# An attention kernel on one core: twelve score visits per unit become ten, with the fills and row visits placed anew

## The chip, the cores and the metric

One core of a Trainium2 chip. The metric is the device time of one launch in microseconds; the kernel before takes 2036.25 us (median of 3 runs, 2035.85 to 2036.71).

## The reference, cut to what matters

The program computes four residual blocks one after the other over x of 2 x 1024 rows of 512: a gated linear recurrence, a feed-forward block, a differential attention and the feed-forward block again. The change is in the attention:

```
q1, q2, k, v = (split_heads(x @ W, 16) for W in (Wq1, Wq2, Wk, Wv))     # 16 heads of 32
p = softmax(where(causal, q @ k.T / sqrt(32), min))                     # for q1 and for q2
y = p1 @ v - sigmoid(x @ Wlam) * (p2 @ v)
return y @ Wo
```

## The kernel before, in words

`phase_rest` (from line 1087) holds the attention and the last feed-forward block. Each engine runs a queue of its own, written out by hand: `@block.tensor`, `.scalar`, `.vector`, `.gpsimd` and `.sync`; they meet at semaphores alone.

**Units.** A turn is one batch and four heads; there are 8 turns (`TURNS`). Each turn is done for two groups of query heads (w = 0 and 1), which makes 16 units (`UNITS`), 0 to 15. A unit works on 1024 queries in two chunks of 512 columns (c = 0, 1) and, of the keys, on tiles kt of 128. `STEPS` (L897) lists the 12 pairs (c, kt) that causality leaves: (0,0) to (0,3), (1,0) to (1,7). On the diagonal a tile covers only the later queries: 512, 384, 256 and 128 columns for the four tiles (`step_width`). One step is one *visit*.

**What TensorE does in a visit** (its loop after L1400), in this order: *scores* (L1339): on the diagonal first 16 small matmuls that put the mask into PSUM (L1349), then for each of the four heads the bias, minus the row maximum, over a ones matrix (L1358, bf16), and keys times queries (L1362, fp32, contraction over 32 rows, the four heads side by side in the array); *weigh* (L1367, L1379): probabilities of the visit before times v, four heads side by side in columns of 32; *rows* (L1311, L1321) in nine of the twelve visits: scores of the next unit in the other orientation, 512 columns per head, from which VectorE takes the row maxima; and *fill* parts (L1235): parts of the projections k and q (L1231) or v (L1271) for the next turn, the softmax denominators (`den`, L1280), the transposed maxima (`neg`, L1284), in the last units transposes for the feed-forward (`norm`, L1289). `output` (L1327, L1335) multiplies with Wo. The last unit has no rows; it takes its denominators with `last_den` (L1384, L1392).

**Which fill stands where** is said by tables: `FIRST_HALF` and `SECOND_HALF` (L927) give for visit i and place 0 or 1 the job that begins there; a projection has four parts (`PARTS`) and takes four places in a row. `FILL_BEFORE_ROWS` puts the place 0 of visits 0 and 4 ahead of the rows. `ROWS` (L900) lists which query tiles and key chunks make up each of the nine row visits, `FIRST_ROW` that they stand in visits 1 to 9. `OUT_AT` places the outputs, `INVERT_AT` VectorE's reciprocals (L1757), `TAKE_AT` GpSimd's `take`.

**PSUM.** Banks 0 to 5 are three pairs that go round in the order of `PAIR_USES` (L1001): each visit's scores take two pairs (a = 0 for heads 0 and 1, a = 1 for heads 2 and 3), its rows two, an output one. Who takes a pair waits for the reader of what stood in it three uses ago:

```
n = PAIR_NTH[use]
kind, u, s, a = PAIR_USES[n - 3]
if kind == "row": pe.wait_ge(row_max, (u * NR + s) * 2 + a + 1)
elif kind == "out": pe.wait_ge(out_added, OUTS.index((u, s)) + 1)
else: pe.wait_ge(exped, (u * NS + s) * 2 + a + 1)
```

Bank 6 collects weigh, bank 7 takes all fills of the steady part.

**The other queues.** ScalarE: for each visit the exps of both halves (L1546), then the copies of finished fills (L1502 to 1531) and of bank 6. VectorE: row maxima (L1701 where no mask is needed, one reduce for a half; L1709 with mask, one per head and piece), reciprocals, `negate` (L1720) and `split` of the maxima, the output's add to x (L1767), in unit 13 statistics (`early_stats`). GpSimd: adds each tile of probabilities to the chunk's total (`add_up`, L1628), `take` (L1640 to 1650) and `spread` (L1613), which makes the bias of the next unit. Three buffers hold probabilities (`prob`), so an exp waits for the add and the weigh of three tiles before. SP issues the loads; `turn_keys` (L1155) copies the two halves of k over each other by DMA, and rows wait for it. `PROLOGUE` jobs and the nine row visits of unit 0 run ahead of unit 0.

## Time and profile before

| what | value |
|---|---|
| median of the runs | 2036.25 us |
| the profiled execution | 2035.62 us, span 2033.8 us |
| TensorE busy, share of the span | 1964.0 us, 97% |
| VectorE, ScalarE, GpSimd busy | 1304.9, 827.8, 864.2 us (64%, 41%, 42%) |
| mean granted TensorE clock | 0.995 of 2.4 GHz |
| start of rows of unit 0, of unit 0, 1, 13, 14, 15 | 775.04, 815.29, 867.37, 1524.11, 1579.40, 1635.69 us |
| start of the last feed-forward block | 1669.6 us |

An execution's own time is somewhat longer than its span from first to last instruction. Busy shares count an engine as busy when any of its instructions runs. Instructions of one kind in a row are merged to one line of the timeline, with a count (x8); fp32 matmuls stand there as two records each.

### The profile page before, as it was taken

Reading aid. Unit: us, or ns where it says so; the run is one execution under the profiler, and the core shown is the slowest. Engines: PE = TensorE matmul, PEld = TensorE weight load, DVE = VectorE, ACT = ScalarE, POOL = GpSimd, SP = SyncE. Lnnn points to the kernel's source line nnn. Section 1 sums busy time; section 2 is a strip of 40 time slices with the busy share of each in tenths; the row PEclk is TensorE's granted clock in tenths of the full one; section 3 lists DMA queues with packets and bytes.
Section 4 is the critical chain, followed back from the end, with each engine's and each line's share of the span. In section 5 each row is a group of like instructions: output and inputs, shape, how many; then the busy total and the mean of one; then the engine's idle time right before and its main releaser. Section 6 shows DMA issues by size and latency. Waiting matters only on the chain.

```text
span 2033.8 us, 36873 instructions
## 1 busy us (share of the span) xinstructions
PE 1964.0 (97%) x15184; PEld 834.6 (41%) x15184; DVE 1304.9 (64%) x2610; ACT 827.8 (41%) x1259; POOL 864.2 (42%) x451
## 2 busy tenths in 40 slices
PE   7998999899999999999999999999998899899999
PEld 3444444444444443333333333333333334344444
DVE  5868686836847456566666666666667635774644
ACT  4435353425444322444444443444434452543431
POOL 3756575800000000667767677777776740000000
PEclk9999999999999999999999999999999999999999
DMA  8111010030000003000101000010000211000001
GB/s 243 32 31 35 28 42 27 21 140 1 1 1 1 1 8 70 23 17 23 22 21 24 12 24 16 22 23 22 2 23 6 62 34 42 1 1 22 21 1 42
DMA packets 71592, 60.21 MB, mean 30 GB/s; under 512 B 37312, under 2 KB 55744, under 8 KB 71168
## 3 DMA queue, kind: packets, MB, share of 16 engines
q1 hardware_dynamic: 64512, 45.27, 7.8%
q10 hardware_dynamic: 6912, 12.59, 2.1%
q8 instruction: 120, 1.97, 0.4%
q14 instruction: 48, 0.39, 0.1%
HBM read 43.02 MB, written 10.62 MB: 26 GB/s over the span
## 4 chain that ended last, share of the span: by engine, by line
PE 53%; DVE 5%; POOL 2%; issue 1%; ACT 1%; DMA 0%; SPq 0%; DVEq 0%; POOLq 0%; ACTq 0%
PE psum L128 9%; PE psum L1231 8%; PE psum L1321 8%; PE psum L1379 6%; PE psum L1362 6%; PE psum L152 5%; PE psum L1271 3%; PE psum L1335 2%; PE psum L1358 2%; POOL b_totals L1628 1%; PE psum L1349 1%; DVE b_maxima L1701 1%; PE psum L1280 1%; DVE psum L1709 1%; DVE x L1767 0%
## 5 line engine op out<-in xcount | busy, mean ns | idle before, releaser
L1628 POOL TENSOR_TENSOR b_totals<-b_totals,b_probs 128x2048 f32<-128x2048 f32 (+3 forms) x100 | 323.9, 3239 | 151.3 <-ACT b_probs L1546 147.7
L1709 DVE CUSTOM_DVE_ANT_0 psum<-psum,b_rest 128x512 f32<-128x512 f32 (+3 forms) x512 | 233.5, 525 | 173.4 <-PE psum L1321 173.3
L447 PE MATMUL psum<-hT,a_win 128*128 128x512 f32 x640 | 292.5, 600 | 0.8 <-ACT hT L574 0.8
L128 PE MATMUL psum<-hT,b_early 128*128 128x512 f16 x1024 | 227.0, 381 | 9.8 <-DVE b_middle L214 6.9
L128 PE MATMUL psum<-hT,W 128*128 128x512 f16 x1024 | 227.5, 382 | 3.6 <-DVE a_win L214 3.6
L1546 ACT ACTIVATE b_probs<-psum 128x1024 f32<-128x1024 f32 (+3 forms) x214 | 153.6, 768 | 150.9 <-PE psum L1362 150.8
L1701 DVE TENSOR_REDUCE b_maxima<-psum 128x2 f32<-128x1024 f32 x128 | 150.8, 1220 | 85.5 <-PE psum L1321 85.2
L1628 POOL TENSOR_TENSOR b_totals<-b_totals,b_rest 128x2048 f32<-128x2048 f32 (+3 forms) x50 | 162.0, 3240 | 68.3 <-ACT b_rest L1546 66.5
L447 PEld LDWEIGHTS psum<-hT,a_win 128*128 128x128 f32 x640 | 120.1, 192 | 130.4 <-issue 129.2
L128 PEld LDWEIGHTS psum<-hT,b_early 128*128 128x128 bf16 x1024 | 99.9, 98 | 133.6 <-DVE b_middle L214 8.8
L128 PEld LDWEIGHTS psum<-hT,W 128*128 128x128 bf16 x1024 | 100.7, 99 | 126.3 <-issue 7.0
L1601 POOL MEMSET b_mask<- 128x128 f32 x1 | 0.2, 205 | 352.3 <-POOLq L279 352.3
L1757 DVE RECIPROCAL b_down<-b_down 128x128 f32<-128x128 f32 x128 | 112.0, 918 | 26.9 <-ACT b_down L1523 26.9
L680 POOL TENSOR_TENSOR a_parts<-a_parts 128x512 bf16<-128x512 bf16 x48 | 60.1, 1251 | 132.7 <-DVE a_parts L754 132.7
L214 DVE SCALAR_TENSOR_TENSOR a_win<-psum,a_win 128x512 f32<-128x512 f32 x64 | 44.1, 690 | 101.2 <-ACT a_win L168 100.2
L1546 ACT ACTIVATE b_totals<-psum 128x1024 f32<-128x1024 f32 x64 | 62.1, 1021 | 106.6 <-PE psum L1362 106.5
L1546 ACT ACTIVATE b_rest<-psum 128x1024 f32<-128x1024 f32 (+3 forms) x106 | 75.1, 760 | 74.3 <-PE psum L1362 74.3
L214 DVE SCALAR_TENSOR_TENSOR b_middle<-psum,lent 128x512 f32<-128x512 f32 x64 | 44.1, 690 | 93.2 <-ACT lent L168 92.6
L152 PE MATMUL psum<-W,a_parts 128*128 128x512 bf16 x256 | 97.0, 379 | 0.0
L152 PE MATMUL psum<-W,a_yo 128*128 128x512 bf16 x256 | 97.0, 379 | 0.0
L152 PE MATMUL psum<-b_down,b_totals 128*128 128x512 bf16 x256 | 97.0, 379 | 0.0
L152 PE MATMUL psum<-b_down,b_probs 128*128 128x512 bf16 x256 | 97.0, 379 | 0.0
(244 smaller groups left out, 3429.5 us busy)
## 6 DMA issues: line engine op xcount, KB each, us to landing
a_parts<-in_w_guT ACTq DMA_DIRECT2D x32, 256.0 KB, 2.8
ternary<-W SPq DMA_DIRECT2D x1, 6144.0 KB, 18.2
a_win<-in_w_inT SPq DMA_DIRECT2D x20, 256.0 KB, 7.2
a_parts<-in_w_pT ACTq DMA_DIRECT2D x16, 256.0 KB, 2.6
b_down<-lam_rows SPq DMA_DIRECT2D x32, 128.0 KB, 2.7
b_early<-ternary SPq DMA_DIRECT2D x8, 512.0 KB, 8.6
out<-x SPq DMA_DIRECT2D x16, 256.0 KB, 2.6
x<-in_x SPq DMA_DIRECT2D x3, 1024.0 KB, 7.9
```

The source lines that it names most:

```text
L128: last = pe.matmul(self.bank[self.up_bank(i, m) + part], self.gu[:, k * 2 * HID + col:k * 2 * HID + col + P], self.hT[:, at:at + BLK], sta ...
L152: last = pe.matmul(self.down_bank(j, t), src[:, m * BLK + t * P:m * BLK + (t + 1) * P], self.wd[:, m * D:(m + 1) * D], start=(m + half == ...
L447: last = pe.matmul(ring(s, j), win[:, at:at + P], core["hT"][:, (i * KT + k) * BLK:(i * KT + k + 1) * BLK], start=(k == 0), stop=(k == KT ...
L1231: last = pe.matmul(to[own, :], weights[:, k * P + own.start:k * P + own.stop], hT[:, at:at + BLK], start=(k == 0), stop=(k == KT - 1))
L1321: last = pe.matmul(to[j // 2][:, j % 2, at:at + width], strip(qT[w][r % 2], j, qt * P, (qt + 1) * P), keys(r, w, j, kc * BLK, kc * BLK + w ...
L1362: last = pe.matmul(to[a][:, j % 2, off:BLK], keys(r, w, j, kt * P, (kt + 1) * P), strip(qT[w][r % 2], j, c * BLK + off, (c + 1) * BLK), st ...
L1379: last = pe.matmul(bank[6][HEAD_AT[j] * HD:(HEAD_AT[j] + 1) * HD, off:BLK], v_rows[r // 2 % 2][:, at:at + HD], held(u, s)[:, j, off:BLK], ...
L1546: act.activation(held(u, s)[:, 2 * a:2 * a + 2, off:BLK], pair_banks(("score", u, s, a))[:, :, off:BLK], ACT.Exp, scale=SCALE).then_inc(ex ...
L1628: pool.tensor_tensor(acc, acc, held(u, s)[:, :, off:BLK], ALU.add).then_inc(summed, 1)
L1701: last = dve.tensor_reduce(maxima[u % 2][:, :].rearrange("p (h q c) -> p h q c", h=HPT, q=QT)[:, 2 * a:2 * a + 2, qt, kc], pair_banks(("ro ...
L1709: last = dve.tensor_tensor_reduce(scores, scores, row_mask[:, BLK - width:BLK], 1.0, -3e38, ALU.add, ALU.max, maxima[u % 2][:, at:at + 1])
L1757: last = dve.reciprocal(rden[k % 2][:, cols], rden[k % 2][:, cols])
```

## The change

`STEPS` gets a new order, in which the tile of 128 columns of each chunk stands right after the one of 384, and `VISITS` joins these two to one visit: both are scored into the same pair (384 columns at 128 to 511, 128 columns at 0 to 127), one after the other, and a half is signalled (`scored`) once its part of the second tile is done. ScalarE reads each tile with an exp of its own, two per half. The next visit weighs both. There are ten visits per unit, 0 to 9. Fills have three places per visit: place 0 always ahead of the rows, 1 and 2 behind them; one entry per part. Rows stand in visits 0 to 8 and in another order, both outputs in visit 9. SP turns the first keys ahead of the weight loads of the start.

```diff
-STEPS = [(c, kt) for c in range(CQ) for kt in range(TPB * (c + 1))]
+STEPS = [(0, 0), (0, 1), (0, 3), (0, 2)] + [(1, kt) for kt in (0, 1, 2, 3, 4, 5, 7, 6)]
 NS = len(STEPS)
-ROWS = [[(0, 0), (2, 0)], [(4, 0)], [(1, 0), (5, 1)], [(5, 0)], [(6, 0)], [(4, 1), (6, 1)], [(3, 0)], [(7, 1)], [(7, 0)]]
+VISITS = [[0], [1, 2], [3], [4], [5], [6], [7], [8], [9, 10], [11]]
+NV = len(VISITS)
+ROWS = [[(0, 0), (2, 0)], [(1, 0), (5, 1)], [(4, 1), (6, 1)], [(4, 0)], [(3, 0)], [(5, 0)], [(6, 0)], [(7, 1)], [(7, 0)]]
 NR = len(ROWS)
-FIRST_ROW = 1
+FIRST_ROW = 0
 def row_pieces(n):
+def score_columns(s):
+    width = BLK - step_width(s)
+    at = 0 if [s] != [v[0] for v in VISITS if s in v] else step_width(s)
+    return slice(at, at + width)
+def exped_by(u, s, a):
+    visit = next(v for v in VISITS if s in v)
+    return (u * NS + visit[0]) * 2 + a * len(visit) + visit.index(s) + 1
-FIRST_HALF = {(0, 0): "k0", (2, 1): "den1", (3, 0): "k1", (5, 1): "den0", (6, 0): "q0", (8, 0): "q1", (10, 1): "neg0"}
-SECOND_HALF = {(0, 0): "q0", (2, 1): "den1", (3, 0): "q1", (5, 1): "den0", (6, 0): "v0", (8, 0): "v1", (10, 1): "neg0"}
-OUT_AT = [{9: 2, 11: 3}, {10: 0, 11: 1}]
-FILL_BEFORE_ROWS = (0, 4)
-NORM_AT = {(3, 0): 0, (4, 0): 1, (6, 0): 2, (7, 0): 3}
-INVERT_AT = {3: (1, 0), 4: (1, 1), 6: (0, 0), 7: (0, 1)}
+FILLS = [{(0, 1): "k0", (0, 2): "k0", (1, 1): "k0", (1, 2): "k0", (2, 0): "den1", (2, 1): "k1", (2, 2): "k1",
+          (3, 1): "k1", (3, 2): "k1", (4, 0): "den0", (4, 1): "q0", (4, 2): "q0", (5, 1): "q0", (6, 1): "q0",
+          (7, 1): "q1", (7, 2): "q1", (8, 1): "q1", (8, 2): "q1", (9, 0): "neg0"}]
+FILLS.append({at: {"k0": "q0", "k1": "q1", "q0": "v0", "q1": "v1"}.get(name, name) for at, name in FILLS[0].items()})
+OUT_AT = [{9: (2, 3)}, {9: (0, 1)}]
+NORM_AT = {(2, 1): 0, (3, 1): 1, (6, 1): 2, (7, 1): 3}
+INVERT_AT = {3: (1, 0), 4: (1, 1), 5: (0, 0), 6: (0, 1)}
 TAKE_AT = {5: 1, 8: 0}
...
+            turn_keys(0)
             sp.dma_start(wv_all[:, :].rearrange("p (k n) -> p k n", k=KT),
                          wv.rearrange("(k p) n -> p k n", p=P)).then_inc(wv_loaded, 16)
...
-            turn_keys(0)
...
-            def scores(u, s):
-                c, kt = STEPS[s]
+            def scores(u, i):
+                steps = VISITS[i]
+                c, kt = STEPS[steps[0]]
                 r, w = divmod(u, 2)
-                off, diagonal = step_width(s), kt >= TPB * c
+                diagonal = kt >= TPB * c
                 to = []
                 if diagonal:
                     for j in range(HPT):
                         if j % 2 == 0:
-                            to.append(take_pair(("score", u, s, j // 2)))
-                        for own in COLUMNS:
-                            pe.matmul(to[j // 2][own, j % 2, off:off + P], ident_b[:, own], later_key[:, :],
-                                      start=True, stop=True)
+                            to.append(take_pair(("score", u, i, j // 2)))
+                        for s in steps:
+                            at = score_columns(s).start
+                            for own in COLUMNS:
+                                pe.matmul(to[j // 2][own, j % 2, at:at + P], ident_b[:, own], later_key[:, :],
+                                          start=s == steps[0], stop=True, skip_group_check=s != steps[0])
                 if kt == 0:
                     pe.wait_ge(bias_ready, u * CQ + c + 1)
-                for a in range(2):
-                    if not diagonal:
-                        to.append(take_pair(("score", u, s, a)))
-                    for j in (2 * a, 2 * a + 1):
-                        rows = slice(j * HD, (j + 1) * HD)
-                        pe.matmul(to[a][:, j % 2, off:BLK], ones_b[rows, :],
-                                  bias[u % 2][rows, c * BLK + off:(c + 1) * BLK],
-                                  start=not diagonal, stop=False, skip_group_check=diagonal)
-                    for j in (2 * a, 2 * a + 1):
-                        last = pe.matmul(to[a][:, j % 2, off:BLK], keys(r, w, j, kt * P, (kt + 1) * P),
-                                         strip(qT[w][r % 2], j, c * BLK + off, (c + 1) * BLK), start=False, stop=True,
-                                         skip_group_check=diagonal)
-                    last.then_inc(scored, 1)
+                for s in steps:
+                    kt, off, cols = STEPS[s][1], step_width(s), score_columns(s)
+                    for a in range(2):
+                        if not diagonal:
+                            to.append(take_pair(("score", u, i, a)))
+                        for j in (2 * a, 2 * a + 1):
+                            rows = slice(j * HD, (j + 1) * HD)
+                            pe.matmul(to[a][:, j % 2, cols], ones_b[rows, :],
+                                      bias[u % 2][rows, c * BLK + off:(c + 1) * BLK],
+                                      start=not diagonal, stop=False, skip_group_check=diagonal)
+                        for j in (2 * a, 2 * a + 1):
+                            last = pe.matmul(to[a][:, j % 2, cols], keys(r, w, j, kt * P, (kt + 1) * P),
+                                             strip(qT[w][r % 2], j, c * BLK + off, (c + 1) * BLK),
+                                             start=False, stop=True, skip_group_check=diagonal)
+                        if s == steps[-1]:
+                            last.then_inc(scored, 1)
...
-                for i in range(NS):
+                for i in range(NV):
                     scores(u, i)
-                    if u == UNITS - 1:
-                        if i == 2:
-                            last_den(0)
-                        if i >= 2:
-                            last_den(i - 1)
-                        weigh(*divmod(u * NS + i - 1, NS))
-                        if i == 1:
-                            fill(*PART_AT[u, 1, 1])
-                        if out_in(u, i):
-                            output(*out_in(u, i))
-                        continue
-                    if u * NS + i:
-                        weigh(*divmod(u * NS + i - 1, NS))
-                    if i in FILL_BEFORE_ROWS and (u, i, 0) in PART_AT:
+                    before = [(u, s) for s in VISITS[i - 1]] if i else [(u - 1, NS - 1)] if u else []
+                    if u == UNITS - 1 and i == 2:
+                        last_den(0)
+                    for at in before:
+                        if at[0] == UNITS - 1 and at[1]:
+                            last_den(at[1])
+                        weigh(*at)
+                    if (u, i, 0) in PART_AT and u < UNITS - 1:
                         fill(*PART_AT[u, i, 0])
                     if row_in(u, i):
                         row(*row_in(u, i))
-                    if i not in FILL_BEFORE_ROWS and (u, i, 0) in PART_AT:
-                        fill(*PART_AT[u, i, 0])
-                    if (u, i, 1) in PART_AT:
-                        fill(*PART_AT[u, i, 1])
-                    if out_in(u, i):
-                        output(*out_in(u, i))
+                    for place in (1, 2):
+                        if (u, i, place) in PART_AT:
+                            fill(*PART_AT[u, i, place])
+                    for out_of in out_in(u, i):
+                        output(*out_of)
...
-            def exps(u, s):
-                c, kt = STEPS[s]
-                off, g = step_width(s), u * NS + s
-                if kt == 0:
-                    if u:
-                        act.wait_ge(filled, NTH[("den", u - 1, c)] + 1)
-                elif summed_by(u, s) > len(prob):
-                    read = summed_by(u, s) - len(prob)
-                    act.wait_ge(summed, min(read, ALL_SUMS))
-                    act.wait_ge(weighed, g - len(prob) + 1)
+            def exps(u, i):
+                for s in VISITS[i]:
+                    c, kt = STEPS[s]
+                    g = u * NS + s
+                    if kt == 0:
+                        if u:
+                            act.wait_ge(filled, NTH[("den", u - 1, c)] + 1)
+                    elif summed_by(u, s) > len(prob):
+                        act.wait_ge(summed, min(summed_by(u, s) - len(prob), ALL_SUMS))
+                        act.wait_ge(weighed, g - len(prob) + 1)
                 for a in range(2):
-                    act.wait_ge(scored, 2 * g + a + 1)
-                    act.activation(held(u, s)[:, 2 * a:2 * a + 2, off:BLK], pair_banks(("score", u, s, a))[:, :, off:BLK],
-                                   ACT.Exp, scale=SCALE).then_inc(exped, 1)
+                    act.wait_ge(scored, 2 * (u * NV + i) + a + 1)
+                    for s in VISITS[i]:
+                        act.activation(held(u, s)[:, 2 * a:2 * a + 2, step_width(s):BLK],
+                                       pair_banks(("score", u, i, a))[:, :, score_columns(s)],
+                                       ACT.Exp, scale=SCALE).then_inc(exped, 1)
...
```

## Rows read from the trace of the kernel before

**Rows 1.** Stretches (units 0; 1-12; 13; 14; 15): us, PE, PEld, DVE, ACT, POOL busy, PEclk.

```profile
815.29:867.37 52.08, 50.02 (x613) 17.68 (x605) 29.61 (x84) 23.50 (x32) 30.70 (x11) 1.00 0.08 22
867.37:1524.11 656.74, 652.02 (x8061) 240.88 (x8065) 422.35 (x1079) 272.45 (x384) 471.95 (x194) 1.00 0.08 19
1524.11:1579.40 55.29, 49.76 (x582) 17.39 (x578) 40.82 (x107) 21.73 (x30) 39.97 (x17) 1.00 0.02 6
1579.40:1635.69 56.29, 48.96 (x533) 18.46 (x529) 38.49 (x97) 25.76 (x35) 42.55 (x19) 0.94 0.27 85
1635.69:1669.60 33.91, 32.39 (x484) 13.17 (x476) 7.99 (x9) 20.09 (x28) 9.67 (x7) 1.00 0.01 1
```

**Rows 2.** Timeline of unit 3, visit 7, tile (1,3): start us, us, engine, line, operation.

```profile
1008.43 0.41 PE L1358 MATMUL psum<-b_last_bias,b_ones_b 32*128 32x512 bf16 x4
...
1009.63 1.07 PE L1379 MATMUL psum<-b_probs,b_early 128*32 128x512 f32 x8
...
1009.81 1.94 ACT L1546 ACTIVATE b_rest<-psum 128x1024 f32<-128x1024 f32 x2 [3.57 <-PE psum L1362]
...
1010.62 1.39 PE L1321 MATMUL psum<-b_early 32*128 32x512 f32 x8
...
1011.94 1.93 PE L1271 MATMUL psum<-b_early,hT 128*32 128x256 f32 x32
...
1013.69 0.41 PE L1349 MATMUL psum<-b_later_key,b_ident_b 128*32 128x128 bf16 x16
...
1014.03 0.41 PE L1358 MATMUL psum<-b_last_bias,b_ones_b 32*128 32x512 bf16 x4
```

**Rows 3.** Timeline of unit 3, rows of visit 5 and scores of visit 6.

```profile
1000.85 1.14 PE L1321 MATMUL psum<-b_early 32*128 32x512 f32 x8
...
1001.92 1.06 PE L1280 MATMUL psum<-b_totals,ones 128*32 128x512 f32 x8
1002.03 2.36 DVE L1701 TENSOR_REDUCE b_maxima<-psum 128x2 f32<-128x1024 f32 x2 [0.60 <-PE psum L1321]
...
1003.31 0.39 PE L1358 MATMUL psum<-b_last_bias,b_ones_b 32*128 32x512 bf16 x2
```

**Rows 4.** Timeline: narrow tiles, scores of 128, weigh of 256, exps of 128 and 384.

```profile
989.82 0.25 PE L1358 MATMUL psum<-b_last_bias,b_ones_b 32*128 32x128 bf16 x4
...
990.27 0.64 PE L1379 MATMUL psum<-b_probs,b_early 128*32 128x256 f32 x8
...
990.84 1.18 PE L1321 MATMUL psum<-b_early 32*128 32x256 f32 x16
...
1029.19 0.66 ACT L1546 ACTIVATE b_probs<-psum 128x256 f32<-128x256 f32 x2 [2.49 <-PE psum L1362]
...
1036.49 1.51 ACT L1546 ACTIVATE b_probs<-psum 128x768 f32<-128x768 f32 x2 [0.82 <-PE psum L1362]
```

**Rows 5.** Timeline of GpSimd in unit 3 and the scores that read its bias.

```profile
1001.70 4.53 POOL L1628 TENSOR_TENSOR b_totals<-b_totals,b_probs 128x2048 f32<-128x2048 f32 x1 [9.24 <-ACT b_probs L1546]
...
1017.43 4.55 POOL L1628 TENSOR_TENSOR b_totals<-b_totals,b_probs 128x2048 f32<-128x2048 f32 x1 [0.74 <-ACT b_probs L1546]
...
1029.28 2.05 POOL L1613 TENSOR_TENSOR b_middle<-b_negT,b_select 128x512 bf16<-128x512 bf16 x2
...
1031.89 0.41 PE L1358 MATMUL psum<-b_middle,b_ones_b 32*128 32x512 bf16 x4
```

**Rows 6.** Timeline ahead of unit 0: last query copy and first rows.

```profile
773.37 0.60 ACT L1505 ACTIVATE b_early<-psum 128x512 f32<-128x512 f32 x1 [2.84 <-PE psum L1231]
...
775.04 1.15 PE L1321 MATMUL psum<-b_early 32*128 32x128 f32 x16 [1.73 <-DMA b_early<-b_early]
```

**Rows 7.** Timeline between units 0 and 1: transpose of the maxima, bias.

```profile
864.44 0.33 PE L1284 MATMUL psum<-ident,b_neg 128*128 128x128 f32 x1
...
867.71 0.41 PE L1358 MATMUL psum<-b_last_bias,b_ones_b 32*128 32x512 bf16 x4 [1.30 <-POOL b_last_bias L1613]
```

**Rows 8.** Timeline of unit 14, rows of visit 1.

```profile
1587.22 2.08 PE L1321 MATMUL psum<-b_middle 32*128 32x128 f32 x12 [2.16 <-ACT b_rest L1546]
```

More of the change, by code:

```diff
@@ L964 @@
 EPILOGUE_BANKS = [7]
[L966 removed]
 PART_AT, ENDING, STEADY = {}, {}, []
[L968 removed]
+for _at in itertools.product(range(UNITS), range(NV), range(3)):
     _job = job_from(*_at)
     if _job:
[L971 to L976 removed]
+        if not STEADY or STEADY[-1] != _job:
+            STEADY.append(_job)
+            _part = 0
+        PART_AT[_at] = (_job, _part)
+        _part += 1
+        if _part == PARTS.get(_job[0], 1):
+            ENDING[_at] = _job
 JOBS = PROLOGUE + STEADY + EPILOGUE
@@ L996, in out_in @@
     r, w = divmod(u, 2)
-    return (r - 1 + w, OUT_AT[w][i]) if i in OUT_AT[w] and 0 < r + w < TURNS else None
+    return [(r - 1 + w, two) for two in OUT_AT[w].get(i, ()) if 0 < r + w < TURNS]
 OUTS = [(r, two) for r in range(TURNS - 1) for two in range(QT // 2)]
@@ L1002 @@
 for _u in range(UNITS):
-    for _i in range(NS):
+    for _i in range(NV):
         PAIR_USES += [("score", _u, _i, a) for a in range(2)]
@@ L1006 @@
             PAIR_USES += [("row", *row_in(_u, _i), a) for a in range(2)]
-        if out_in(_u, _i):
-            PAIR_USES.append(("out", *out_in(_u, _i), 0))
+        PAIR_USES += [("out", *_out, 0) for _out in out_in(_u, _i)]
 PAIR_NTH = {use: n for n, use in enumerate(PAIR_USES)}
@@ L1554, in _ @@
             for u in range(UNITS):
-                for i in range(NS):
+                for i in range(NV):
                     exps(u, i)
@@ L1563, in _ @@
                         act.activation(e_root[:, :], e_var[:, :], ACT.Sqrt).then_inc(early_root, 1)
-                    for place in range(2):
+                    for place in range(3):
                         if (u, i, place) in ENDING:
                             copy_out(ENDING[u, i, place])
+                        if place == 0 and CHUNK_LAST[0] in VISITS[i - 1]:
+                            weigh_out(u, 0)
             weigh_out(UNITS - 1, 1)
@@ L1818, in _ @@
             for u in range(UNITS):
-                for i in range(NS):
-                    if u == UNITS - 2 and NORM_AT.get((i + 1, 0), 2) < 2:
-                        early_turn(0, NORM_AT[i + 1, 0])
-                    if i == NS - 2 and u + 1 < UNITS:
+                for i in range(NV):
+                    if u == UNITS - 2 and NORM_AT.get((i + 1, 1), 2) < 2:
+                        early_turn(0, NORM_AT[i + 1, 1])
+                    if i == NV - 1 and u + 1 < UNITS:
                         negate(u + 1)
@@ L1825, in _ @@
                         row(*row_in(u, i))
-                    for place in range(2):
+                    for place in range(3):
                         if (u, i, place) in ENDING and ON_DVE[NTH[ENDING[u, i, place]]]:
                             finish(ENDING[u, i, place])
-                    if out_in(u, i):
-                        add_out(*out_in(u, i))
+                    for out_of in out_in(u, i):
+                        add_out(*out_of)
                     if i in INVERT_AT:
```

25 lines of the change are left out of this document (8 added, 17 removed).

## The prediction

> **What bounds the kernel now.** I read the stretches first: the attention stage by units of work [rows 1]. Units 1 to 12 take 656.74 us, 54.73 each, and TensorE is busy for 652.02 of it, VectorE for 422, GpSimd for 472, ScalarE for 272. So TensorE's queue is the path, and the question is what stands in that queue. Busy does not mean undelayed: four narrow matmuls share the array, and if two of them wait, the other two still count as busy. I therefore time by the distance from one group's start to the next group's start.
>
> The timeline of a full visit [rows 2] gives such distances: scores with bias 1.20 (1008.43 to 1009.63), weigh 1.00, rows 1.32, a fill of two parts 1.75, a mask 0.34. The same row group costs 1.07 elsewhere (1000.85 to 1001.92) [rows 3]. The missing 0.25 is a wait. The six PSUM banks go round as three pairs, and the second pair of a row visit is the one that held the first half of the scores of the same visit; it comes free when ScalarE has done the first exp. In [rows 2] the exps start 1.38 after the bias and two take 1.94, so the first is over about 2.40 after the bias; the row group reached its turn at 2.19. Hence a rule for everything below: **the rows' second half cannot start before 2.45 after the bias start of a full score, and what is missing adds in full.**
>
> A second wait comes from VectorE: it starts on the rows' first half 1.18 after their start and needs 1.18 for it (1000.85, 1002.03, two reduces 2.36), so the next visit's second score half starts 2.46 after the rows (1003.31) [rows 3].
>
> **The change, part by part, in a steady unit.** Widths: scores of 128 columns take 0.45, a weigh of 256 takes 0.57 [rows 4]; between these and the full ones I interpolate: scores of 256 and 384 0.70 and 0.95, weigh of 384 0.78. Two fill parts with a mask behind them took 1.75, so one takes 0.87; a weigh is as large, and with rows behind it took 1.00 [rows 2]. So a change between column groups (weigh, fill, denominator, mask) and row groups (scores, rows) costs about 0.13; a weigh with a fill behind it is 0.86, two fill parts with scores behind them 1.86.
>
> *Removed:* two visits. Rows visits have four such changes each and the others two: nine times four and three times two before, nine times four and once two after, 4 x 0.13 = 0.5 us a unit. No column of work goes away.
>
> *Moved:* rows 0 now stand in visit 0 behind a weigh of 256 (0.57) where a fill stood, rows 3 in visit 3 again behind a weigh of 256, where 128-wide weigh and a fill part stood before. Both reach their turn 1.77 after the bias: 0.68 of wait each. The denominators at place 0 of visits 2 and 4 stand ahead of the rows and cover the wait there.
>
> *Merged visits (1 and 8):* the first half is signalled only with the narrow tile's scores. Exps start at 0.82 + 0.64 = 1.46 after the bias, the 384-wide one takes 1.51/2 and the 128-wide one 0.66/2 [rows 4], so the first half is free at 2.6; the rows' turn is at 1.29 + 1.00: 0.32 each.
>
> The ten visits (mask, scores, weigh, denominator, rows with their wait, fills):
> 0: 0.34+1.20+0.57+1.76+1.74 = 5.61.
> 1: 0.57+1.29+1.00+1.40+1.74 = 6.00.
> 2: 0.34+0.70+0.89+1.00+1.08+1.86 = 5.87.
> 3: 1.20+0.57+1.76+1.86 = 5.39.
> 4: 1.20+0.86+1.00+1.08+1.86 = 6.00.
> 5: 1.20+1.00+1.33+1.00 = 4.53.
> 6: its second score half waits 0.14 for VectorE: 4.38.
> 7: its mask waits 0.33 for VectorE (2.46 after rows that have one fill part behind them): 0.67+1.20+1.00+1.33+1.74 = 5.94.
> 8: as 1, 6.00.
> 9: 0.34+0.70+1.02, transpose of the maxima 0.26, both outputs together 3.46: 5.78.
> Sum 55.5 for 54.73: about **+0.7 a unit, +8.9 for twelve**. The saved changes are in it; the waits behind the first exp (2.3 a unit for 0.5 now) eat them and more.
>
> **Covers that I checked.** *GpSimd:* from its add of tile (1,1) to the spread of the next bias are 27.6 us, and the scores that read it follow at 1031.89, 1.5 behind its first half [rows 5]. After the change visits 4 to 9 and a mask are 32.9 us; the spread's half is done 3.4+27.6+1.1 = 32.1 behind visit 4's start, 0.8 ahead. The take of the previous unit now waits for the second reciprocal (VectorE ends at 8.6, GpSimd comes at 8.0), but the 0.74 that GpSimd idles before tile (1,4) [rows 5] takes that up. *ScalarE's copies:* the denominator's copy ends about 0.15 before the next fill part wants its bank in visit 4. *VectorE's negation:* over 0.8 before its transpose. *The outputs, now back to back:* the first one's add is over 3.2 after it begins, the next masks' second half comes at 3.6. *Probability buffers:* there are three, and in visit 8 two exps need one each, the second that of tile (1,3); GpSimd has added that by 21 behind visit 4's start at the latest, the exps come at 22.5. I cost these at nothing; if they are gone, each costs up to 0.5 a unit. Late next would be the GpSimd spread.
>
> On the price of ScalarE's two narrow exps the rows say 1.08 for the pair [rows 4]. The Trainium skill (ScalarE: Activation LUTs, Rules for kernel authors) budgets about 0.3 us for each ACTIVATE plus 0.83 ns an element; that speaks against splitting a half over two exps, and by it a merged visit would wait some 0.36 more, the sum 8.7 more. The row's duration is what I use.
>
> **The other units.** *Start:* SP turns the first keys right after one load. Rows 0 waited for those transfers until 775.04; the last query copy ends at 773.97 [rows 6], so they start there: -1.0. The new row order makes VectorE slower on rows 1 and 2, +0.4, and quicker later, -0.2: together **-0.8**. The loads queued behind on SP are wanted 20 us later. *Unit 0* has no outputs to put between the transpose and the next bias. From the one to the other were 3.27 us, and 1.30 of it was a wait although a whole visit stood between [rows 7]; now nothing stands between: 2.67. Without a first weigh, rows 0 also wait 1.22. My sum of its visits with that is 53.7 for 52.08: **+1.6**. *Unit 13* has no fills behind visit 3. Rows follow rows at 2.46 (2.63 after the sums with mask) +1.20+1.00, masks added: rows 4 at 25.9, then 30.8, 35.4, 40.3, 45.6, the end at 53.7, plus 0.5 as the spread is then late: 54.3 for 55.29, **-1.0**. *Unit 14* has no fills but the four transposes (`norm`), one place after the rows now, and took 56.29. Its second visit waited for exps behind ScalarE's root and two table loads (2.16 idle at 1587.22 [rows 8]), and the mean granted clock was 0.94 [rows 1], so part of it ran at 1.2 GHz. Now rows 0 are in front of that wait. GpSimd's two turned rows (2.1 each) fall into its idle time before tile (1,1). By the same steps (its first masks after visit 0 wait for VectorE until 5.6) rows stand at 2.1, 8.1, 13.8, 18.3, 23.9, 28.7, 33.3, 38.3, 43.5, the end at 51.9: **-4.4**, between 0 and -6, since the clock may fall again. *Unit 15* has no rows; two fewer visits and shorter waits: **-1.3**, between 0 and -2.
>
> Sum: -0.8+1.6+8.9-1.0-4.4-1.3 = +3.0. Against the profiled execution (2035.62) that is 2038.6; the median of the runs is 0.63 above it, so 2039.3. About 0.2%, 4.1 us, is what can be told from no change.
>
> Bounds. Each wait of 0.68 and 0.32 is at least what full visits show with later turns (nothing, if the exp came sooner) and at most 0.3 longer if the signal of the merged half comes later; I take the arithmetic. On the whole 0.3 a unit to either side, 4 us, and 3 us for units 13 to 15.
>
> **Rivals.** *A: my forecast*, 2034 to 2043, chance 0.50. *B: faster.* The changes of tile shape are saved, and rows wait no longer than they do now, 0.5 a unit, because fill parts or earlier exps cover them: 1.8 less in 12 units, 2017; if half of that comes, 2028. For it: TensorE is busy 99%, and the end stretch gains. Against it: the wait at 1010.62 fits the exp to 0.05 us, and visits 0 and 3 have less in front. 0.22. The Trainium skill (TensorEngine Tiling, Key Properties) states that a change of tiling mode drains the engine; the 0.13 agrees, and so few changes are saved that it stays at 0.5 a unit. *C: slower.* GpSimd becomes the bound at the unit's edge: if its chain slips by 1.3 (0.8 slack gone), the first scores of each unit wait 0.5, 13 units 6.5: 2046. It decides from a spread that ends later than 32.9 behind visit 4's start. For: 0.8 of slack, a new wait for the reciprocal. Against: 0.74 idle ahead of it. 0.20. *D: the end stretch gives nothing*, and the clock falls in unit 14: 2044. 0.08.
>
> **Numbers.** Likeliest 2039. The range 2029 to 2047 leaves out the far half of B and longer slips. Faster by over 0.2%: B nearly whole, 0.21; within: most of A, 0.39; slower: the rest, 0.40.
>
> **What would show it.** A steady unit of 55.5; row groups of 1.76 in visits 0 and 3 and 1.40 in 1 and 8; rows 0 at 774; unit 14 near 52 with the clock at full; no wait of the bias on GpSimd but behind unit 0. Units at or under 54.2 would prove me wrong on the exp wait; a bias wait in each unit would be C.

## The result and the profile after

| | before | after |
|---|---|---|
| median, runs taken side by side | 2036.37 us (6) | 2044.55 us (6) |
| profiled execution: its time, its span | 2035.62, 2033.8 us | 2043.03, 2041.2 us |
| mean granted TensorE clock | 0.995 | 0.994 |

The ratio is 1.0038, its 95% interval 1.0028 to 1.0048: **slower by 0.4%**, 8.2 us. The forecast was 2039 in a range of 2029 to 2047, with chances of 0.40 for slower by over 0.2%, 0.39 for no change that can be told and 0.21 for faster. The time lies in the range, some 5.5 us above the likeliest value. The reasons for it do not hold everywhere, as the stretches of the two profiled executions show (their spans differ by 7.4 us).

The changed kernel, the same stretches as in [rows 1] with unit 1 by itself (us; PE, PEld, DVE, ACT, POOL busy; PEclk), units 0, 1, 2 to 12, 13, 14 and 15:

```profile
813.55:867.30 53.75, 49.99 (x613) 18.72 (x605) 29.72 (x84) 23.18 (x32) 30.68 (x11) 1.00 0.08 21
867.30:923.48 56.18, 55.76 (x689) 22.05 (x693) 34.23 (x89) 22.39 (x32) 39.81 (x18) 0.97 0.08 16
923.48:1529.51 606.03, 603.28 (x7375) 229.32 (x7371) 390.01 (x990) 246.27 (x352) 432.22 (x177) 1.00 0.09 20
1529.51:1589.71 60.20, 52.57 (x597) 19.16 (x589) 45.30 (x108) 21.41 (x30) 38.68 (x16) 0.94 0.02 6
1589.71:1646.29 56.58, 49.96 (x529) 19.60 (x529) 39.48 (x98) 25.59 (x35) 43.28 (x19) 0.94 0.28 85
1646.29:1678.44 32.15, 31.26 (x464) 12.89 (x464) 7.16 (x9) 19.79 (x28) 9.99 (x8) 1.00 0.01 2
```

Against [rows 1], in us of the span (after less before):

| stretch | forecast | measured |
|---|---|---|
| up to unit 0's start (815.29 to 813.55) | -0.8 | -1.7, of it -1.2 ahead of the last query copy, where nothing is changed |
| unit 0 | +1.6 | +1.7 |
| units 1 to 12 (656.74) | +8.9 | +5.5: 4.0 in units 2 to 12, 1.4 in unit 1 |
| unit 13 | -1.0 | **+4.9** |
| unit 14 | -4.4 | **+0.3** |
| unit 15 | -1.3 | -1.8 |
| the feed-forward part | 0 | -1.4 |
| sum | +3.0 | +7.4, which is 2041.2 less 2033.8 |

Units 2 to 12 take 55.09 each for 54.73, and the granted clock does not fall in them. Unit 3 of the changed kernel on TensorE, the lines that answer to [rows 2, 4]: visit 0, the merged visit 1, visit 3.

```profile
978.90 0.41 PE L1379 MATMUL psum<-b_last_bias,b_ones_b 32*128 32x512 bf16 x4
...
980.10 0.64 PE L1401 MATMUL psum<-b_rest,b_early 128*32 128x256 f32 x8
980.67 0.49 PE L1337 MATMUL psum<-b_early 32*128 32x128 f32 x4
981.33 1.14 PE L1337 MATMUL psum<-b_early 32*128 32x128 f32 x12 [0.18 <-ACT b_totals L1561]
982.40 1.92 PE L1247 MATMUL psum<-hT,lent 128*32 128x512 f32 x16
...
984.70 0.35 PE L1379 MATMUL psum<-b_last_bias,b_ones_b 32*128 32x384 bf16 x4
...
985.97 1.07 PE L1401 MATMUL psum<-b_totals,b_early 128*32 128x512 f32 x8
986.96 1.46 PE L1337 MATMUL psum<-b_early 32*128 32x256 f32 x16
988.35 1.92 PE L1247 MATMUL psum<-hT,lent 128*32 128x512 f32 x16
...
997.66 1.79 PE L1337 MATMUL psum<-b_early 32*128 32x512 f32 x8
999.38 1.92 PE L1247 MATMUL psum<-hT,lent 128*32 128x512 f32 x16
```

The rows of visit 0 take 1.73 from start to start (980.67 to 982.40), of visit 3 1.72, of the merged visit 1.39: forecast 1.76, 1.76 and 1.40. The profile notes only 0.18 of visit 0's as a wait; that the rest is one too is read from the distance, 0.66 above the 1.07 of a row group that does not wait [rows 3].

The unit's edge, which answers to [rows 5]: GpSimd's spread of the next bias, and the scores that read it.

```profile
1032.39 2.05 POOL L1629 TENSOR_TENSOR b_middle<-b_negT,b_select 128x512 bf16<-128x512 bf16 x2
1034.01 0.41 PE L1379 MATMUL psum<-b_middle,b_ones_b 32*128 32x512 bf16 x4
```

Visit 4 began at 1001.24, so the first half was spread 32.2 behind it (forecast 32.1) and the scores came at 32.8 (forecast 32.9). The profile shows no wait of the scores for it in units 2 to 12: rival C is out.

The other answering rows of the changed kernel: the last query copy and first rows [rows 6], the bias of unit 1 [rows 7] and the rows of visit 1 in unit 14 [rows 8].

```profile
772.18 0.60 ACT L1520 ACTIVATE b_early<-psum 128x512 f32<-128x512 f32 x1 [2.83 <-PE psum L1247]
773.03 1.15 PE L1337 MATMUL psum<-b_early 32*128 32x128 f32 x16 [0.91 <-ACT b_early L1520]
...
867.64 0.63 PE L1379 MATMUL psum<-b_last_bias,b_ones_b 32*128 32x512 bf16 x4 [2.60 <-POOL b_last_bias L1629]
868.04 1.94 PE L1383 MATMUL psum<-b_early 32*128 32x512 f32 x8
869.91 0.97 PE L1401 MATMUL psum<-b_probs,b_early 128*32 128x256 f32 x8
...
1599.36 1.13 PE L1337 MATMUL psum<-b_middle 32*128 32x256 f32 x12 [0.90 <-ACT b_probs L1561]
```

In unit 1 the scores and the bias take 2.27 (867.64 to 869.91) where a steady unit has 1.20: behind the wait of 2.60 TensorE runs at the lower clock level. Where unit 13 lost 4.9 stands in these lines between the rows of visit 4 and the scores of visit 5:

```profile
1555.59 4.50 POOL L1644 TENSOR_TENSOR b_totals<-b_totals,b_probs 128x2048 f32<-128x2048 f32 x1 [9.21 <-ACT b_probs L1561]
1555.66 4.46 DVE L1796 TENSOR_SCALAR b_e_var<-b_e_mv 128x8 f32<-128x8 f32 x1
...
1560.31 0.70 DVE L1725 CUSTOM_DVE_ANT_0 psum<-psum,b_rest 128x512 f32<-128x512 f32 x1 [0.19 <-DVE b_e_var L1796]
...
1561.77 0.61 PE L1379 MATMUL psum<-b_last_bias,b_ones_b 32*128 32x512 bf16 x2 [4.32 <-DVE b_maxima L1725]
```

VectorE's variance step of 8 columns took 4.46 us. It began 0.07 behind GpSimd's add (1555.59) and ended with it (1560.12 and 1560.09). The row maxima behind it came late, the scores waited 4.32 for them, and the clock fell. In the kernel before the same step ran while GpSimd was idle; its next add came 4.0 later:

```profile
1546.03 0.17 DVE L1780 TENSOR_SCALAR b_e_var<-b_e_mv 128x8 f32<-128x8 f32 x1
...
1550.04 4.53 POOL L1628 TENSOR_TENSOR b_totals<-b_totals,b_probs 128x2048 f32<-128x2048 f32 x1 [10.20 <-ACT b_probs L1546]
```

Measured from the start of unit 13, the add hardly moved: 25.9 before, 26.1 after. The step moved, from 21.9 to 26.1. The four parts of the statistics are tied to the numbers of the visits, 0 to 3, a line that the change leaves as it is. With two visits joined to one, visit 3 lies later in the unit.

The low clock of the changed kernel, at the edge of units 0 and 1, in unit 13 and in unit 14 (PEclk 0.50, that is 1.2 of 2.4 GHz):

```profile
867.30:870.60 3.30, 2.96 (x20) 0.90 (x20) 0.00 (x0) 0.53 (x1) 3.16 (x4) 0.50 0.02 5
1560.20:1566.90 6.70, 5.13 (x19) 1.38 (x23) 4.32 (x10) 1.02 (x1) 2.14 (x2) 0.50 0.00 0
1601.20:1607.90 6.70, 6.07 (x56) 2.62 (x60) 2.60 (x13) 1.68 (x3) 5.94 (x3) 0.50 0.00 0
```

### The profile page after: what moved, and what is told of

Same layout as the page of the kernel before. It is cut to its first block, busy times and chain, and to the rows that moved or that the text cites. A ratio compares the mean times of both kernels' runs of the same rounds, so it can differ in the third digit from the quotient of the medians.

```text
span 2041.2 us, 36832 instructions
## 1 busy us (share of the span) xinstructions
PE 1968.4 (96%) x15143; PEld 847.7 (42%) x15184; DVE 1311.7 (64%) x2610; ACT 822.9 (40%) x1259; POOL 864.1 (42%) x451
## 4 chain that ended last, share of the span: by engine, by line
PE 53%; DVE 4%; POOL 3%; ACT 2%; issue 1%; DVEq 0%; POOLq 0%; ACTq 0%
PE psum L129 9%; PE psum L1337 8%; PE psum L1247 8%; PE psum L1401 6%; PE psum L1383 6%; PE psum L153 5%; PE psum L1287 3%; PE psum L1379 2%; POOL b_totals L1644 2%; PE psum L1351 2%; PE psum L1368 1%; PE psum L1296 1%; DVE b_maxima L1717 1%; ACT b_totals L1561 1%; DVE psum L1725 1%
## 5 line engine op out<-in xcount | busy, mean ns | idle before, releaser
L1337 PE MATMUL psum<-b_early 32*128 32x512 f32 (+3 forms) x768 | 100.8, 522 | 4.4 <-ACT b_totals L1561 2.5
L1337 PE MATMUL psum<-b_middle 32*128 32x512 f32 (+3 forms) x768 | 101.3, 528 | 2.1 <-ACT b_totals L1561 1.2
```

Source lines behind the costliest of these rows:

```text
L1337: last = pe.matmul(to[j // 2][:, j % 2, at:at + width], strip(qT[w][r % 2], j, qt * P, (qt + 1) * P), keys(r, w, j, kc * BLK, kc * BLK + w ...
```

## The experiments

Times are medians, the ratio is to the kernel before, run beside it on the same chip. Stretches and lines are from one profiled execution of each kernel.

**1. The root without VectorE's step** (on the changed kernel).

```
- v.settle()
- v.did(dve.tensor_scalar(e_var, e_mv[:, 1:2*QT:2], LN_EPS, 1/(UP*UP), ALU.add, ALU.mult))
- act.activation(e_root, e_var, ACT.Sqrt)
+ act.activation(e_root, e_mv[:, 1:2*QT:2], ACT.Sqrt, bias=ln_up[:, 0:1], scale=1/(UP*UP))   # ln_up: a column of LN_EPS/(UP*UP)
```

> The changed kernel, with VectorE's one tensor_scalar of 128x8 that ended the statistics of unit 13 left out and folded into ScalarE's square root (scale and bias). Theory (VectorE's tensor_scalar stood 4.46 us because GpSimd's add of 4.50 us had begun 0.07 us before it and held the SBUF port pair; TensorE then idled 4.3 us and its clock fell for 6.8 us): the scores of unit 13, visit 5, take about 2.6 instead of 7.80 us, unit 13 about 54.3 instead of 60.2, no stretch of the lower clock near its middle; 2037 to 2039 us for 2044.5. Rival (VectorE had too much work in that visit, the long instruction is only where it shows): leaving out 0.17 us of work saves under 0.5 us, 2044.

2037.81 us, ratio 1.0004 (0.9995 to 1.0013). Units 13 and 14 of this kernel:

```profile
1530.79:1585.30 54.51, 50.17 (x597) 18.87 (x589) 40.86 (x107) 21.42 (x30) 38.71 (x16) 1.00 0.02 6
1585.30:1639.07 53.77, 47.14 (x529) 18.59 (x529) 39.47 (x98) 25.69 (x35) 43.30 (x19) 1.00 0.30 89
```

Unit 13 falls by 5.7 to 54.51; 54.3 was forecast. Unit 14 falls by 2.8, as its low stretch does not come this time. Units 2 to 12 are the same to 0.01. One instruction of 8 columns cost most of the loss: of the 8.2 us over the kernel before, 1.2 are left (2037.81 to 2036.63).

**2. The end of the statistics one visit earlier** (on the changed kernel): the fourth part, which ends with the variance step, goes from visit 3 to visit 2. The instruction stays, its moment changes.

```
- if u == UNITS - 3 and i < QT // 2: early_stats(i)
+ if u == UNITS - 3 and i < 3: early_stats(i)
+     if i == 2: early_stats(3)
```

> The changed kernel with the last part of the statistics of unit 13 one visit earlier, right behind the third part, where GpSimd idles; the instructions are the same. Port theory: the 128x8 tensor_scalar takes 0.17 us there, and the same 6 to 8 us come back as in the run without it, 2037 to 2039. Rival (too much work for VectorE): 1.3 us more of it now stand before the rows of visit 3, whose first half would be late by up to 0.5; at best 1 us is saved, 2043 to 2045.

2038.45 us, ratio 1.0006 (0.9997 to 1.0015), unit 13 55.20. VectorE's step is over four us before GpSimd's next add:

```profile
1553.02 0.17 DVE L1796 TENSOR_SCALAR b_e_var<-b_e_mv 128x8 f32<-128x8 f32 x1
...
1557.31 4.52 POOL L1644 TENSOR_TENSOR b_totals<-b_totals,b_probs 128x2048 f32<-128x2048 f32 x1 [9.22 <-ACT b_probs L1561]
```

Unit 14 kept its low stretch (56.53). So it is not the instruction by itself but that it meets the add.

**3. A fill part ahead of the rows** in visits 0 and 3 (on the changed kernel).

```
- (0, 1), (0, 2): "k0"   (3, 1), (3, 2): "k1"
+ (0, 0), (0, 1): "k0"   (3, 0), (3, 1): "k1"
```

> The changed kernel with one of the two fill parts of visits 0 and 3 ahead of the rows, as in the kernel before. Theory (rows' second half waits until 2.45 us after the bias start for the first exp; the next scores' second half or mask waits 2.46 after the rows start, 2.8 for the eight-piece rows of visit 0): rows of 1.73 become 1.08 in both; behind visit 0 the mask then waits 0.6, behind visit 3 the scores wait 0.38: a unit 0.2 to 0.4 us shorter, units 1 to 12 -3 to -4 us. Rival (the 0.65 us are no wait for the exp but a cost of rows behind a weigh of 256): rows get cheaper and nothing waits behind them, -0.9 a unit, or rows stay at 1.73 and the unit gets longer by the extra change of shape.

2039.69 us, ratio 1.0013 (1.0004 to 1.0022). Units 2 to 12 come to 54.85, 0.24 less each, as expected. Visit 3 with 4, whose start moves, takes 11.05 for 11.34, while visit 0 with 1 takes 11.57 for 11.53: there the next mask waits for VectorE, whose maxima follow the rows. By chance this kernel also varies the meeting of experiment 1:

```profile
1551.57 4.50 POOL L1644 TENSOR_TENSOR b_totals<-b_totals,b_probs 128x2048 f32<-128x2048 f32 x1 [8.57 <-ACT b_probs L1561]
...
1552.48 0.64 DVE L1794 BATCH_NORM_AGGREGATE b_e_mv<-b_e_stats 128x2 f32<-128x6 f32 x8
1553.16 2.94 DVE L1796 TENSOR_SCALAR b_e_var<-b_e_mv 128x8 f32<-128x8 f32 x1
1556.29 0.70 DVE L1725 CUSTOM_DVE_ANT_0 psum<-psum,b_rest 128x512 f32<-128x512 f32 x1 [0.18 <-DVE b_e_var L1796]
```

The step began 1.59 behind the add and took 2.94; it ended 0.03 behind the add's end again (1556.10, 1556.07). Its length is what is left of the add. The eight aggregates of the statistics just before it ran beside the same add and took 0.64, as they did in the kernel before with GpSimd idle: not every instruction of VectorE is held.

**4. Rows ahead of the fill in one full visit more**, visit 4 (on the kernel before).

```
- FILL_BEFORE_ROWS = (0, 4)
+ FILL_BEFORE_ROWS = (0,)
```

> The kernel before with one table entry less: in visit 4 the fill part that stood ahead of the rows goes behind them, so that, as in visits 0 and 3 of the changed kernel, rows follow a short weigh. Same work, one change of tile shape less. Theory (rows' second half cannot start before 2.45 us after the bias start): rows' turn comes at 1.57, they take 1.96 instead of 1.08, and the next scores save their 0.36 of wait: visits 4 and 5 together +0.54, units 1 to 12 +6.5 us, 2043. Rival (nothing but the change of shape counts): -0.13 a unit and the saved 0.36, so 5 to 6 us faster.

2043.03 us, ratio 1.0037 (1.0024 to 1.0050). Units 2 to 12 take 55.35 for 54.73. Unit 3 of this kernel, visit 4:

```profile
994.71 0.41 PE L1358 MATMUL psum<-b_last_bias,b_ones_b 32*128 32x512 bf16 x4
...
996.26 2.01 PE L1321 MATMUL psum<-b_early 32*128 32x512 f32 x8
998.20 1.93 PE L1231 MATMUL psum<-hT,lent 128*32 128x512 f32 x16
```

The rows start 1.55 after the bias and take 1.94 for 1.07, so the next group starts 3.49 after the bias. Had the change of shape been all that counts, the kernel would have been faster. This is the rule of the exp, in the kernel before and with the rows of one visit moved. It alone costs more per unit (0.62) than the whole change (0.36).

**5. The narrow tiles unmerged**, with every other part of the change kept (on the changed kernel).

```
- VISITS with (384, 128) pairs: ten
+ VISITS = [[s] for s in range(NS)]: twelve, fills, rows and outputs at the same scores as after
```

> The changed kernel with the two merged visits taken apart again: twelve score visits, but the new step order, the new row order and the new places of fills, rows and outputs (the first of each two split visits has neither rows nor fills). Theory (the merge saves four changes of tile shape, 0.5 us a unit, and pays 0.31 us of wait in rows twice for the exps of the joined half): by the group times visits 1 and 8 cost 0.56 more each, the weighs behind them 0.65 less, so a unit comes out 0.1 to 0.2 shorter than the 55.1 now; units 1 to 12 together -1 to -3 us. Rival (the merge saves its 0.5 us net): a unit 0.5 longer, +6 us over twelve units. Unit 13 meets GpSimd's add at another moment, so its 5 us may be there or not: the verdict is read from units 2 to 12.

2040.86 us, ratio 1.0016 (1.0007 to 1.0025). Units 2 to 12 take 55.15, so the merge is worth 0.06 a unit, where 0.1 to 0.2 the other way was expected and 0.5 by the rival; unit 15 takes 34.08 for 32.15, so there it is worth 1.9. The variance step stands 20.6 behind the start of unit 13 here, as visit 3 is again the fourth of twelve, and the add at 26.1: it met no add (0.17), and unit 13 took 54.52. Its profiled span is 2040.3 all the same, in part because it reaches the first rows 4.3 later than the changed kernel (777.28 for 773.03), through code that is the same.

**6. The keys' turn alone** (on the kernel before): `turn_keys(0)` ahead of the last load.

> The kernel before with one part of the change alone: SP turns the first keys ahead of the weight loads. Theory (the first rows waited for those transfers until 775.04 while the last query copy was over at 773.97): the first rows start 15.67 - 1.0 = 14.6 us after the first projection instead of 15.67, all behind is as before, the time 1.0 us less. Rival (the loads that now queue behind the wait come late and cost it again): the rows or the fills of the start wait elsewhere, no gain.

2035.05 us, ratio 0.9994 (0.9985 to 1.0003). The first rows start 0.85 after the start of the last query copy for 1.67 in [rows 6]: 0.8 of the 1.0 expected. Units 0 to 13 and 15 keep their lengths to 0.02, unit 14 took 0.3 more. The median alone cannot tell it from no change.

**7. The gap between units 0 and 1 filled** (on the changed kernel).

```
+ if u == 1 and i == 0 and j == 0:
+     for _ in range(12):
+         pe.matmul(to[0][:, 0], ident_b, bias[0][:, 0:BLK], start=True, stop=True)
```

> The changed kernel with 12 matmuls of 128x512 (bf16) put into the gap in which TensorE waits 2.6 us for the bias of unit 1; they write a bank that the mask starts anew. Theory (the granted clock went to 1.2 GHz for 3.4 us right behind this gap and that costs 1.4 us in unit 1): no such stretch near 867, unit 1 takes 54.8 to 55.1 instead of 56.18, the time 1.2 us less. Rival (the longer scores and weigh there are the bias coming in two halves): unit 1 stays at 56.2, or longer by what of the 2.56 us of extra work does not fit the gap.

2044.46 us, ratio 1.0042 (1.0028 to 1.0055). The same moment and the whole of unit 1:

```profile
867.66:870.96 3.30, 3.11 (x50) 1.57 (x52) 0.00 (x0) 1.60 (x2) 3.16 (x4) 1.00 0.02 5
...
867.66:922.78 55.12, 54.86 (x706) 21.97 (x710) 34.25 (x89) 22.39 (x32) 39.86 (x18) 1.00 0.09 16
```

Unit 1 is a steady unit again (55.12 for 56.18), so its surplus was the clock behind the gap. The median did not move, 1.2 less was expected. In the profiled execution the feed-forward part has a low stretch and takes 364.5 for 362.8; whether filling the gap brought it there is not shown.

This kernel keeps VectorE's variance step, and it meets the add once more: 4.45 us from 1554.98, beside an add of 4.49 from 1554.90.

**8. Experiment 1 with the part ahead in visit 3 only.**

> The changed kernel with two of the edits: no tensor_scalar of VectorE in unit 13 (ScalarE's root takes scale and bias) and one fill part ahead of the rows in visit 3 only. Theory: 2037.8 of the run with the first edit, less 0.28 for each unit 1 to 12 (rows 1.08 instead of 1.73, one more change of shape, 0.36 of wait in the next scores), -3.4: 2034.4, 0.1% under the kernel before. Rival (the two gains overlap or the next waits grow): 2037 to 2038.

2034.48 us for the 2034.4 expected, ratio 0.9996 (0.9987 to 1.0004), not to be told from the kernel before. Units 2 to 12 take 54.81, unit 13 54.79, unit 14 55.14 with a low stretch.

**9. The table load off the path** (on the kernel of experiment 8). ScalarE in unit 14 of the changed kernel loads a table for the root and the exp's table back, the second one (1596.93) only when the scores of the next exp are there:

```profile
1593.87 1.28 ACT L1577 ACT_TABLE_LOAD   x1
1595.16 0.21 ACT L1577 ACTIVATE b_e_root<-b_e_var 128x8 f32<-128x8 f32 x1
1596.93 1.28 ACT L1561 ACT_TABLE_LOAD   x1 [1.56 <-PE psum L1383]
```

```
  act.activation(e_root, ..., ACT.Sqrt, ...)
+ act.activation(warm, l_root[:, 0:1], ACT.Exp)
```

> The changed kernel with the root's add left to ScalarE, k1's second part a visit early (both as in e8_root_part), and one thing more: a dummy exp of one column on ScalarE right behind the root in unit 14's first visit, its result unused. The question is what unit 14 still loses. In the changed kernel the table load behind the root (1.28 us) is issued only when the next score's exp is free to start, so that the rows of visit 1 wait 2.66 us. Theory 1 (the load lies on the path): with the dummy exp the load falls beside the scores, the rows of visit 1 wait 1.2 to 1.5 us, unit 14 comes to 53.3 to 54.1 us (55.1 in e8_root_part, 3.4 us of it at the low clock), and the run to about 2033. Theory 2 (the load is hidden by the wait for the scores, unit 14's surplus is the clock alone): the rows wait as before and unit 14 stays at 55 us. Theory 3: the load falls into the first visit's own exps, whose rows then wait 1.3 longer there, and nothing is won.

2031.88 us, ratio 0.9978 (0.9969 to 0.9987). ScalarE, TensorE and unit 14 of this kernel:

```profile
1587.62 1.28 ACT L1581 ACT_TABLE_LOAD   x1
1588.91 0.20 ACT L1581 ACTIVATE b_warm<-b_l_root 128x1 f32<-128x1 f32 x1
...
1589.90 1.46 PE L1339 MATMUL psum<-b_middle 32*128 32x256 f32 x16
...
1581.86:1634.43 52.57, 46.77 (x529) 18.60 (x529) 39.39 (x98) 25.87 (x36) 43.31 (x19) 1.00 0.29 91
```

The load starts 0.02 behind the root, the rows of visit 1 take 1.38 from start to start for 2.66 in the changed kernel, and unit 14 comes to 52.57, with no low stretch. Theory 1 held, and the unit is below its 53.3 to 54.1.

**10. Experiment 9 with the gap filled** as in experiment 7.

> e9_table with the twelve matmuls of e6_busy_gap, ahead of the bias's masks of unit 1's first visit, which fill the gap of 2.6 us at the edge of units 0 and 1 (their result is overwritten by the bias's own start, so nothing computed changes). Theory 1: unit 1 comes to 55.0 to 55.2 us at the high clock, as it did in e6_busy_gap, against 56.2, and no low stretch takes its place further on: 1.1 us less than e9_table, about 2032, and faster than the kernel before by 0.15 to 0.2%. Theory 2, by e6_busy_gap's own result, in which the median did not move although unit 1 was 1.1 us shorter: a low stretch comes elsewhere (the feed-forward part had one) and the median is e9_table's within 1 us.

2030.69 us, ratio 0.9977 (0.9967 to 0.9987). Unit 1 took 54.83 for 55.85, but the medians differ by 1.2 within runs that scatter by 4 (2029.15 to 2033.01): not settled.

**11. The kernel before with the same care**: keys turned first, and root and dummy exp ahead of unit 14's first exp.

```
  for i in range(NS):
+     if u == UNITS - 2 and i == 0:
+         act.wait_ge(early_var, 1)
+         act.activation(e_root, e_var, ACT.Sqrt).then_inc(early_root, 1)
+         act.activation(warm, l_root[:, 0:1], ACT.Exp)
      exps(u, i)
```

> The kernel before with two edits that have nothing to do with the change's visits: the first keys turned ahead of the loads (as in e3_turn_first, 0.8 us measured), and ScalarE's root put ahead of the first exp of unit 14, with the dummy exp of e9_table behind it. In the kernel before ScalarE stands idle for 3.39 us ahead of that exp, while root and the two table loads (1.28 and 0.21 and 1.28) stand behind it and hold the rows of visit 1 for 2.16 us. The question is whether the gain of e10_all needs the change at all. Theory 1 (the gain is the repairs'): the rows of visit 1 wait under 0.3 us, the clock stays at its high level in unit 14, which comes from 56.3 to 51.5 to 53.5 us, and the run to about 2031 to 2032: as fast as e10_all, and the change of the visits is worth nothing by itself. Theory 2 (the change's new order, rows 0 ahead of the root, is what helps unit 14): unit 14 stays above 54.5 us and the run above 2033.5.

**2029.50 us**, ratio 0.9965 (0.9952 to 0.9979), the lowest of all, though the interval overlaps those of experiments 9 and 10, which ran on another chip. ScalarE and TensorE ahead of visit 1, and unit 14:

```profile
1575.88 1.28 ACT L1559 ACT_TABLE_LOAD   x1
1577.17 0.21 ACT L1559 ACTIVATE b_e_root<-b_e_var 128x8 f32<-128x8 f32 x1
1577.40 1.28 ACT L1560 ACT_TABLE_LOAD   x1
...
1582.73 1.15 PE L1322 MATMUL psum<-b_middle 32*128 32x128 f32 x16
...
1577.55:1629.40 51.85, 46.20 (x534) 17.54 (x530) 38.52 (x97) 24.31 (x34) 42.57 (x19) 1.00 0.29 93
```

Both loads lie in ScalarE's idle time, the wait of 2.16 in [rows 8] is gone, the clock stays up, and unit 14 takes 51.85 for 56.29. Theory 1 held: the gain of experiment 10 is the repairs'. In the profiled executions this kernel is 6.1 us shorter than the kernel before: 4.4 of it lie in unit 14, 0.8 between the last query copy and the first rows, and 1.0 ahead of that copy, where nothing is changed. From first rows to the feed-forward part this kernel takes 890.1 us (773.24 to 1663.32), that of experiment 10 891.2 (773.82 to 1665.06). Unrepaired, the change costs 8.2 us; with both sides repaired no gain of it is to be seen.

## Why the prediction was right and where it was wrong

**The steady unit: mechanism right, size off.** All ten visits lie within 0.08 of their forecasts, and the waits behind the first exp came as worked out. Experiment 4 shows the mechanism in the kernel before, experiment 3 shows it in the changed one. The rows of a merged visit took 1.39 for 1.40, which bears out the price of the narrow exps, 1.08 a pair. But the sum was 55.50 for 55.09 measured, +0.77 for +0.36 against the 54.73 of before: nine of the ten visits were put 0.01 to 0.08 too long. On a difference of 0.36 that is more than half, and the forecast was 3.4 us too high over twelve units. (Two sums of the prediction are slips: 0.77 times twelve is 9.2, not 8.9, and 53.7 plus 0.5 in unit 13 is 54.2, not 54.3.) The merge by itself was put at 0.5 saved and 0.64 paid, and measured 0.06 gained: right that it is next to nothing, wrong in its sign.

**Start, unit 0, unit 15:** the keys' turn gave 0.8 (experiment 6) and unit 0 begins 0.3 later behind the first rows, -0.5 for -0.8; the other 1.2 lie ahead of the last query copy, which starts anywhere from 771.8 to 776.4 in kernels with the same code up to there. Unit 0 was put at +1.6 and measured +1.7, unit 15 -1.3 and -1.8. Right.

**Unit 13, the step that failed** (-1.0 forecast, +4.9 measured). "Rows follow rows at 2.46 (2.63 after the sums with mask) +1.20+1.00" priced VectorE's queue by the maxima alone. The queue also holds the statistics' steps, and joining the visits moved one of them, by 4.2 us within the unit, to the very moment at which GpSimd's add begins. I had checked who waits for GpSimd, and never which VectorE instruction runs beside it. It cost 5.7 us of unit 13 (experiment 1). Without it the unit took 54.51, close to the 54.3 of the sum. The Trainium skill (SBUF — State Buffer, Who interferes with whom) states the rule: VectorE and GpSimd share a port pair under an exclusive lock, held for the whole instruction by whoever starts first; VectorE needs it in its two-port modes or with two inputs from SBUF, and `tensor_scalar` is named among the operations that can enter these modes. The rows here agree: 0.17 with GpSimd idle, 4.46, 4.45 and 2.94 with the add running, ending with it each time. I could have applied it ahead of the result, and did not.

**Unit 14, the second step that failed** (-4.4 forecast, +0.3 measured). "By the same steps [...] the end at 51.9: -4.4" took the wait behind the root as gone because rows 0 now stand ahead of it. But the rows of visit 1 still wait: the second table load is issued only when the scores of visit 1 are there, and the exps that free the rows' bank stand behind it. The low clock came too. Experiment 9 takes both away and gives 52.57, 0.7 above my sum of 51.9. Experiment 1, with the load on the path and without the low stretch, took 53.77; the changed kernel, with both, 56.58. So of the 4.7 that the sum lacked the load is 1.2, the low clock 2.8, and the rest 0.7.

**Unit 1, not foreseen:** I priced the gap behind unit 0 at its length, 2.67 (measured 2.60), and not the low clock behind it, 1.1 more (experiment 7).

**The rivals.** B (faster by the saved shape changes) was out by its own test, since units stayed above 54.2. C's chain held its slack. D came as written for unit 14 (+0.3, the clock low), but its 2044, my 2039.3 and the 4.4 of unit 14, was met by another sum: it has unit 13 at -1.0 and units 1 to 12 at +8.9. That the total lies in my range owes something to luck: 3.4 too much in units 1 to 12 stand against 10.6 too little in units 13 and 14, and 2.6 us that the profiled execution won lie in parts in which nothing is changed (1.2 ahead of the last query copy, 1.4 in the feed-forward part).

**What stays open.** When the clock falls in unit 14: experiments 1, 5, 9, 10 and 11 kept it up (PEclk 1.00), 7 and 8 in part (0.97), the others and both kernels did not (0.94), and experiments 1 and 2 have the same waits in its first visits. Why the feed-forward part takes 362.6 to 362.8 in the changed kernel and experiments 2, 3, 5, 9 and 10, and 364.2 to 364.5 in all others, is seen (one low stretch in the latter, as from 1737 in the kernel before, none in the former); nothing in that part was changed, and the cause stays open.

## What to carry to other kernels

When work is tied to the number of a visit, joining visits moves it, though its line stays as it was. When a change shifts one engine's work against another's, list for each long GpSimd instruction which VectorE instructions now fall beside it, the tiny ones of rare units too: here 0.17 us became the rest of a 4.5 us add, with the whole queue behind it. Look for the places where the kernel already waits (a root between two table loads, a transfer queued behind a load) before its regular part is rebuilt: edits of a few lines in two places gave 7.1 us in the medians (2036.58 to 2029.50), 5.2 of it in the stretches that they touch, where the rebuilt visits gave nothing. And a difference of two sums of ten terms needs terms taken from rows of the same shape where there are any, since here errors of 0.04 made half of the result.

## What the runs showed of the hardware

- A `tensor_scalar` of 8 columns on VectorE took 0.17 us with GpSimd idle. When an add of 4.5 us had begun on GpSimd 0.07, 0.08 or 1.59 before it, it took what was left of the add: 4.46, 4.45, 2.94 us. The aggregates beside the same add kept their 0.64.
- A wait of TensorE can cost beyond its own length: behind the gap of 2.60 the same scores took 2.27 for 1.20 at the granted clock of 0.50, and unit 1 was 1.1 longer than with the gap filled.
- A low stretch can come in code that is the same: the feed-forward part had one in experiment 7 and none in the changed kernel, and took 1.7 more with it.
- A table load is issued when the next activation's wait is met, and not as soon as ScalarE is free: 1.56 us of idle time stood in front of it in the changed kernel, and a dummy exp of 0.20 us moved it there. The Trainium skill (ScalarE: Activation LUTs, What ACT_TABLE_LOAD costs) puts a switch at 1.28 for the load and another 1.38 for a drain; here the root started 1.29 behind the load's start, with no drain to be seen.
